# One decoder kernel: the second cross attention as one stream of eight half-batch units

## The chip, the cores and the metric

The kernel runs on one core of one Trainium2 chip. The metric is the time of one launch in microseconds (us), as the device reports it; less is better. TensorE (PE) multiplies, VectorE (DVE), ScalarE (ACT) and GpSimd (POOL) work on the elements, and SyncE (SP) issues the DMAs of this stage. Each engine runs its own list of instructions in order and waits on semaphores for the others.

## The reference

Two decoder layers on 4 batches of 512 tokens with 512 features. Each layer is self attention, cross attention and a feed-forward part, each with its residual and layer norm. The change is in the cross attention of the second layer alone (32 heads of 16 features, context of 256 features):

```python
q = (x @ Wq).reshape(b, n, N_HEADS, HEAD_DIM)
k, v = jnp.split(ctx @ Wkv, 2, axis=-1)
q = apply_axial_rope(q, pos_map)
k = apply_axial_rope(k, ctx_pos_map)
logits = jnp.einsum('bqhd,bkhd->bhqk', q, k) * scale
w = jax.nn.softmax(logits, axis=-1)
attn = jnp.einsum('bhqk,bkhd->bqhd', w, v)
attn = attn.reshape(b, n, N_HEADS * HEAD_DIM)
return attn @ Wout + bout
# afterwards: x = _layernorm(x + ...)
```

## The kernel before

`cross_attention_1` is one stage between two barriers. A loop (`Fori(0, B)` on every engine, B = 4) goes over the batches, and each batch has three parts.

**The head** prepares all 32 heads. PE turns the rows of x and of the context into columns (`turn_tile`, line 116), then projects q tile by tile (L1570) and k and v (L1575). DVE applies the rotary embedding (L1744 to L1749: multiply, two swapped multiplies, add). q and k are split into a high and a low part, since the score matmuls run in the one-pass format fp32r: ACT copies the high part (L1672), and DVE (L1729) and POOL (L1797) subtract to get half of the low part each. PE turns the split rows (L116, "x_ident_r,x_split") and ACT copies them out (L1666) into `q_cols` and `k_cols`, where each head takes 64 rows.

**The steps** are 64 pieces of work that a `plan` orders. One step has the scores of two heads for 128 queries (L1599: two matmuls on the upper and the lower 64 rows of the array, into one pair of PSUM banks) and DVE's row maximum over both banks (L1762). 14 steps later the same two heads are multiplied the other way round (L1618), with the negated maximum in the added rows, and ACT takes the exponential (L1688). Every second step has a "values" piece (L1626: four matmuls of 17 columns side by side in the array). Every 8 steps (a group of four heads) add the turning of the maxima (DVE L1768 and L1770, PE L1608, ACT L1680, four DMAs into `q_cols`) and the way back of the group's result (ACT copy L1693, PE L116, DVE L1776 and L1778). The PSUM banks are two pairs for scores, a ring of three for the weights (a bank is free again when its exponential is done) and one for the values.

**The tail** turns `feats`, multiplies by Wout (L1645), adds the bias (L73), the residual (L77), and normalises (L85 to L96). Only then does the head of the next batch begin.

## Time and profile before

| | us |
|---|---|
| median of 3 runs | 3331.95 (3326.03 to 3333.94) |
| profiled execution: its own time | 3331.01 |
| profiled execution: span | 3329.3 |
| PE busy in the span | 2951.1 (89%) |
| DVE, ACT, POOL busy | 2053.9, 1524.7, 243.0 |
| the changed stage, from 2285.3 to 3014.5 | 729.2 |

The rows are of three kinds: a table of busy times in stretches (here one stretch is one batch, from the first score matmul to the next batch's first); single instructions in order of time, where "x4" joins neighbours of the same kind and the difference of two starts says what a group takes; and groups of equal instructions with their mean duration. A PE duration contains the time through the array, so a group's cost is read from start to start. A plain fp32 matmul shows as two instructions, an fp32r one as one.

### The profile page before, as it was taken

Reading aid. Unit: us, or ns where it says so; the run is one execution under the profiler, and the core shown is the slowest. Engines: PE = TensorE matmul, PEld = TensorE weight load, DVE = VectorE, ACT = ScalarE, POOL = GpSimd, SP = SyncE. Lnnn points to the kernel's source line nnn. Section 1 sums busy time; section 2 is a strip of 40 time slices with the busy share of each in tenths; the row PEclk is TensorE's granted clock in tenths of the full one; section 3 lists DMA queues with packets and bytes.
Section 4 is the critical chain, followed back from the end, with each engine's and each line's share of the span. In section 5 each row is a group of like instructions: output and inputs, shape, how many; then the busy total and the mean of one; then the engine's idle time right before and its main releaser. Section 6 shows DMA issues by size and latency. Waiting matters only on the chain. (4 is left out here: it accounts for less than half of the span.)

```text
span 3329.3 us, 45585 instructions
## 1 busy us (share of the span) xinstructions
PE 2951.1 (89%) x13653; PEld 1768.8 (53%) x13676; DVE 2053.9 (62%) x3875; ACT 1524.7 (46%) x3177; POOL 243.0 (7%) x234
## 2 busy tenths in 40 slices
PE   8999978799999996998998999997898888984787
PEld 4455444336999994655655655654334343432343
DVE  5666645444566565756756856854747575766776
ACT  4445422223555552443543542633556556574444
POOL 0000020002000000101102102101000000000000
PEclk9999989898999998999999999998898989895899
DMA  3000023000000001100000000001000000003000
GB/s 120 13 13 0 13 76 103 31 22 9 12 13 11 11 10 70 76 1 14 1 1 14 1 1 13 1 1 61 2 21 2 21 2 21 2 2 152 7 19 25
DMA packets 43029, 82.10 MB, mean 25 GB/s; under 512 B 6256, under 2 KB 21377, under 8 KB 39393
## 3 DMA queue, kind: packets, MB, share of 16 engines
q1 hardware_dynamic: 39952, 71.60, 6.0%
q0 software_dynamic: 2896, 8.31, 0.8%
q8 instruction: 88, 1.44, 0.2%
q14 instruction: 93, 0.75, 0.1%
HBM read 55.25 MB, written 4.19 MB: 18 GB/s over the span
## 5 line engine op out<-in xcount | busy, mean ns | idle before, releaser
L1232 ACT ACTIVATE a_probs<-bank,a_neg_max 128x128 f32<-128x128 f32 (+3 forms) x256 | 138.6, 542 | 390.6 <-DVE a_neg_max L1335 390.6
L1762 DVE TENSOR_REDUCE x_neg_max<-bank 128x2 f32<-128x1024 f32 x256 | 298.9, 1217 | 28.4 <-PE bank L1599 28.4
L116 PE MATMUL bank<-all_ident,a_probs 128*128 128x128 f32 x1216 | 198.4, 276 | 57.5 <-ACT a_probs_t L1248 39.5
L116 PEld LDWEIGHTS bank<-all_ident,a_probs 128*128 128x128 f32 x1216 | 151.0, 142 | 159.6 <-ACT a_probs L1238 61.5
L1190 PE MATMUL bank<-a_wo,a_att_cols 128*128 128x512 f32 x512 | 226.9, 594 | 1.2 <-DVE a_att_cols L1300 0.9
L955 DVE TENSOR_TENSOR moe_hid_low<-moe_hid,moe_hid_high 128x512 fp32r<-128x512 f32 x168 | 116.3, 692 | 177.1 <-ACT moe_hid_high L825 169.8
L1618 PE MATMUL bank<-x_q_cols,x_k_cols 64*128 64x512 f32 x512 | 160.9, 446 | 35.7 <-ACT x_x_rows L1688 12.7
L753 PE MATMUL bank<-moe_w_high,moe_hid_low 128*128 128x256 f32 x672 | 190.2, 283 | 0.0
L753 PE MATMUL bank<-moe_w_low,moe_hid_high 128*128 128x256 f32 x672 | 190.1, 283 | 0.0
L753 PE MATMUL bank<-moe_w_high,moe_hid_high 128*128 128x256 f32 x672 | 189.3, 282 | 0.1
L1165 PE MATMUL bank<-a_k_cols,a_q_cols 128*128 128x128 f32 (+3 forms) x512 | 176.8, 434 | 0.0
L819 ACT ACTIVATE moe_hid<-bank,moe_b_now 128x512 f32<-128x512 f32 x168 | 115.7, 688 | 122.3 <-PE bank L731 122.3
L1599 PE MATMUL bank<-x_k_cols,x_q_cols 64*128 64x512 f32 x512 | 137.5, 531 | 29.8 <-DVE x_neg_max L1762 21.1
L1131 PE MATMUL bank<-a_x_high,a_w_high 128*128 128x512 f32 x320 | 138.2, 432 | 23.5 <-DVE a_k_cols L1287 11.9
L825 ACT CAST moe_hid_high<-moe_hid 128x512 fp32r<-128x512 f32 x168 | 104.4, 621 | 112.4 <-PE bank L753 112.2
L1190 PEld LDWEIGHTS bank<-a_wo,a_att_cols 128*128 128x128 f32 x512 | 94.2, 190 | 106.6 <-issue 104.4
L1177 PE MATMUL bank<-a_probs_t,a_v_rows 128*128 128x512 f32 (+3 forms) x512 | 148.6, 433 | 0.0
L1238 ACT ACTIVATE a_probs<-a_probs,a_inv_sum 128x128 f32<-128x128 f32 (+3 forms) x256 | 144.8, 565 | 7.6 <-DVE a_inv_sum L1340 7.6
L947 DVE SCALAR_TENSOR_TENSOR moe_acc<-bank,moe_gate_now,moe_acc 128x256 f32<-128x256 f32 x336 | 139.4, 477 | 13.2 <-issue 12.1
L1309 DVE TENSOR_TENSOR all_x_tok<-bank,all_x_tok 128x512 f32 (+1 forms) x64 | 44.2, 691 | 159.6 <-PE bank L1190 159.6
L1335 DVE TENSOR_REDUCE a_neg_max<-bank 128x1 f32<-128x128 f32 (+3 forms) x256 | 125.7, 491 | 19.1 <-issue 0.5
L731 PE MATMUL bank<-moe_gh_high,moe_w_high 128*128 128x512 f32 x336 | 133.7, 398 | 2.1 <-DVEq L938 2.1
(353 smaller groups left out, 6629.2 us busy)
## 6 DMA issues: line engine op xcount, KB each, us to landing
x_x_rows<-all_x_tok SPq DMA_DIRECT2D x8, 1024.0 KB, 6.3
moe_w<-in_L_ffn_e_w SPq DMA_DIRECT2D x40, 128.0 KB, 2.2
all_x_tok<-in_x SPq DMA_DIRECT2D x1, 4096.0 KB, 17.7
x_c_rows<-in_ctx SPq DMA_DIRECT2D x8, 512.0 KB, 4.5
moe_x_rows<-all_x_tok SPq DMA_DIRECT2D x4, 1024.0 KB, 4.7
a_probs<-all_x_tok SPq DMA_DIRECT2D x4, 1024.0 KB, 4.5
a_wqkv<-in_L_attn_Wqkv SPq DMA_DIRECT2D x1, 4096.0 KB, 20.2
a_wo<-in_L_attn_Wo SPq DMA_DIRECT2D x1, 4096.0 KB, 30.0
```

Of the source, the lines that this page charges most:

```text
L116: last = pe.transpose(bank[:, c * P:(c + 1) * P], rows[:, c * P:(c + 1) * P], ident)
L753: last = pe.matmul(to, h[:, c, tokens], weight[:, slot, c, :], start=c == j == n == 0, stop=c == 1 and n == 2, skip_group_check=True)
L947: last = dve.scalar_tensor_tensor(acc[:, t, :], mm[b % 2 * 2 + half][:, j * LATENT:(j + 1) * LATENT], gate_now[:, slot, t:t + 1], acc[:, t ...
L1131: last = pe.matmul(mm[g % 2], weight[:, p % 2, k, :], x[:, k, :], start=n == 0, stop=n == 3 * KD - 1)
L1165: pe.matmul(sc[n % 4][:, 0:t], q_cols[:, h % 2, j * P:t], k_cols[:, h // GROUP, 0:t], start=True, stop=True).then_inc(s.sc.full, 1)
L1177: last = pe.matmul(mm[g % 2][:, c * P:], v_rows[:, c, kv * HD1:(kv + 1) * HD1], probs_t[:, n % 2, c, c * P:], start=c == 0, stop=c == NT - 1)
L1190: last = pe.matmul(mm[g % 2], att_cols[:, h % HALF_HEADS, j * P:(j + 1) * P], wo[:, h, :], start=h == first, stop=h == end - 1)
L1232: act.activation(probs[:, n % SLOTS, 0:t], sc[n % 4][:, 0:t], ACT.Exp, bias=neg_max[:, n:n + 1], accum_out=row_sum[:, n:n + 1]).then_inc(s ...
L1238: act.activation(probs[:, i % SLOTS, 0:t1], probs[:, i % SLOTS, 0:t1], ACT.Copy, scale=inv_sum[:, i:i + 1]).then_inc(s.probs_ready, 1)
L1599: last = pe.matmul(pair_banks[slot % 2][:, u, :], q_cols[rows, pair, j * P:(j + 1) * P], k_cols[rows, pair, :], start=True, stop=True)
L1618: pe.matmul(weight_banks[slot % 3], k_cols[rows, pair, c * P:(c + 1) * P], q_cols[rows, pair, :], start=True, stop=True).then_inc(s.weight ...
L1762: dve.tensor_reduce(neg_max[:, g % 2, j, 2 * pair:2 * pair + 2], pair_banks[slot % 2], AX.X, ALU.max, negate=True) \
```

## The change

The loop over batches is gone. The stage is eight units (u), a half batch of 16 heads each, with 32 steps per unit, all in one `plan` from step -34 on that every engine walks. A unit's steps are as before: scores, weights 14 steps later, values, shift, back. Between them stand the next unit's preparation (v = u + 1): q in two pieces (two tiles of 128 tokens by 256 features each) at steps 0 to 6, k at 8 and 12, v at 16 and 18, the rotary pieces, the "high" (ACT) and "low" (POOL) parts, 16 "pad" turnings at the odd steps from 7 to 17 and at 19 to 25, and the last finished batch's turning of feats, output matmuls and layer norm at steps 20 to 30 of the unit after it and 20 to 27 of the one after that. The last batch's output comes after its last step.

The PSUM banks are dealt anew: a ring of three single banks for scores (so one maximum per head), two for weights (three before), one for values, and two work banks that all preparation shares; a piece takes whichever is emptied first. The buffers of exponentials are two (three before). All of the low part and the bias are POOL's. x is turned straight from `x_tok`, so its reload (1 MB per batch) is gone; the context comes in halves into one buffer, so the second half of batch 0 is loaded behind the weights.

On PE in the steady part, the kernel before, one step with values (x1_k_cols,x1_q_cols are scores; x1_q_cols,x1_k_cols weights):

```order
L1596 REGISTER_ALU
L1599 MATMUL bank<-x1_k_cols,x1_q_cols 128x512 x2
L1617 REGISTER_ALU
L1618 MATMUL bank<-x1_q_cols,x1_k_cols 128x512
L1617 REGISTER_ALU
L1618 MATMUL bank<-x1_q_cols,x1_k_cols 128x512
L1626 MATMUL bank<-x1_x_rows,x1_v_rows 17x512 x4
```

The change, unit 2, steps 22 to 24:

```order
L116 MATMUL bank<-all_ident,x1_feats 128x128 x8
L1704 MATMUL bank<-x1_k_cols,x1_q_cols 128x512 x2
L1715 MATMUL bank<-x1_q_cols,x1_k_cols 128x512 x2
L1737 MATMUL bank<-x1_weights,x1_v_rows 17x512 x4
L116 MATMUL bank<-x1_ident_r,x1_split 128x128 x8
L1704 MATMUL bank<-x1_k_cols,x1_q_cols 128x512 x2
L1715 MATMUL bank<-x1_q_cols,x1_k_cols 128x512 x2
L1663 MATMUL bank<-x1_wout,x1_feats_t 128x512 x2
```

Between scores and weights of neighbouring steps there now stand turnings, projections or output matmuls. On DVE, the kernel before, from the end of one group to its way back:

```order
L1762 TENSOR_REDUCE x1_neg_max<-bank 128x2
L1767 REGISTER_ALU
L1768 CAST x1_shift<-x1_neg_max 128x16
L1770 TENSOR_TENSOR x1_shift<-x1_neg_max,x1_shift 128x16
L1761 REGISTER_ALU
L1762 TENSOR_REDUCE x1_neg_max<-bank 128x2
L1761 REGISTER_ALU
L1762 TENSOR_REDUCE x1_neg_max<-bank 128x2
L1774 REGISTER_ALU
L1776 RECIPROCAL x1_inv_sum<-bank 128x16
L1778 TENSOR_TENSOR x1_feats<-bank,x1_inv_sum 128x4x64
```

The change, steps 9 to 11 of a unit:

```order
L1857 TENSOR_REDUCE x1_neg_max<-bank 128x1 x2
L1875 RECIPROCAL x1_inv_sum<-bank 128x16
L1877 TENSOR_TENSOR x1_feats<-bank,x1_inv_sum 128x4x64
L1899 TENSOR_TENSOR x1_rot<-x1_rot,x1_swapped 128x512
L1890 TENSOR_TENSOR x1_rot<-bank,x1_cos 128x512
L1857 TENSOR_REDUCE x1_neg_max<-bank 128x1 x2
L1894 TENSOR_TENSOR x1_swapped<-bank,x1_sin 128x256 x2
```

The rotary add of q's second piece now stands behind the group's reciprocal, which waits for PE's turning, and two more instructions follow before the next maxima.

The diff, cut to its core:

```diff
-    PAIRS = HEADS // 2
+    UNITS, UH = 2 * B, HEADS // 2
+    UD = UH * HD
+    PAIRS = UH // 2
...
-    SHIFT_SPLIT, SHIFT_TURN = -1, 1
-    T_LAG, V_LAG, BACK_LAG = 14, 2, 4
+    LAG = 14
...
+    first, last_step = -STEPS - 2, STEPS * (UNITS + 2)
+    plan = {i: [] for i in range(first, last_step)}
...
+    for u in range(UNITS):
+        for n in range(STEPS):
+            plan[u * STEPS + n].append(("scores", u, n))
+    for u in range(UNITS):
+        for g in range(GROUPS):
+            plan[u * STEPS + (g + 1) * GS - 1].append(("shift_split", u, g))
+        for n in range(STEPS):
+            plan[u * STEPS + n + LAG].append(("weights", u, n))
+    for u in range(UNITS):
+        for g in range(GROUPS):
+            plan[u * STEPS + (g + 1) * GS + 1].append(("shift_turn", u, g))
+        for n in range(CHUNKS):
+            plan[u * STEPS + LAG + 2 * n + 3].append(("values", u, n))
+        for g in range(GROUPS):
+            plan[u * STEPS + LAG + (g + 1) * GS + 1].append(("copy", u, g))
+            plan[u * STEPS + LAG + (g + 1) * GS + 3].append(("back", u, g))
+
+    def project(piece, where, subs, done):
+
+        for i, step in enumerate(where):
+            for sub in range(i * subs, (i + 1) * subs):
+                plan[step].append(("fill", piece, sub))
+        for kind, step in done:
+            plan[step].append((kind, piece))
...
+    def turn(piece, step):
+        plan[step] += [("fill", piece, 0), ("evac", piece)]
...
+    for v in range(UNITS):
+        at = (v - 1) * STEPS
+        b, hf = divmod(v, 2)
+        if v == 0:
+            prepare_rows(b, at, (-2, -2, -2, -2))
+            prepare_context(b, at, (-1, -1))
+        project(("q", v, 0), (at, at + 2), 2, [("rope_mul", at + 3), ("rope_swap", at + 4), ("rope_add", at + 5), ("high", at + 5), ("low", at + 6)])
+        project(("q", v, 1), (at + 4, at + 6), 2, [("rope_mul", at + 7), ("rope_swap", at + 8), ("rope_add", at + 9), ("high", at + 9), ("low", at + 10)])
+        project(("k", v, 0), (at + 8,), 2, [("rope_mul", at + 9), ("rope_swap", at + 10), ("rope_add", at + 11)])
+        project(("k", v, 1), (at + 12,), 2, [("rope_mul", at + 13), ("rope_swap", at + 14)])
+        for pad, steps in ((0, (7, 9, 11, 13)), (1, (15, 15, 17, 17))):
+            for j, step in enumerate(steps):
+                turn(("pad", v, "q", j, pad), at + step)
+        for kind, step in (("high", 16), ("low", 17)):
+            plan[at + step].append((kind, ("k", v, 0)))
+        plan[at + 15].append(("rope_add", ("k", v, 1)))
+        for kind, step in (("high", 18), ("low", 19)):
+            plan[at + step].append((kind, ("k", v, 1)))
+        for n, step in enumerate((19, 20, 21, 21, 23, 23, 25, 25)):
+            turn(("pad", v, "k", n // 4 * 2 + n % 2, n // 2 % 2), at + step)
+        project(("v", v, 0), (at + 16,), 2, [("value_copy", at + 17)])
+        project(("v", v, 1), (at + 18,), 2, [("value_copy", at + 19)])
+        if hf == 0:
+            for j in range(NT):
+                plan[at + 20 + j].append(("bias", b, j))
+        if hf == 1 and b + 1 < B:
+            prepare_rows(b + 1, at, (9, 11, 13, 13))
+            prepare_context(b + 1, at, (27, 29))
+    for b in range(B):
+        at = (2 * b + 2) * STEPS
+        for j, step in enumerate((20, 20, 22, 22)):
+            turn(("feats", b, j), at + step)
+        late = STEPS if b + 1 < B else 0
+        for j, steps in enumerate(((24, 26), (28, 30), (late + 20, late + 22), (late + 24, late + 26)) if late else ((24, 24), (25, 25), (26, 26), (27, 27))):
+            project(("out", b, j), [at + i for i in steps], 2, [("ln_add", at + steps[-1] + 1)])
+        end = at + (late + 27 if late else 28)
+        plan[end].append(("ln_var", b))
+        for j in range(NT):
+            plan[end + 1 + j // 2].append(("ln_norm", b, j))
...
+            bank = 0 if busy[0] < busy[1] else 1
...
+            work_at[piece[1]] = bank, uses[bank]
+            uses[bank] += 1
+            busy[bank] = consumed[piece[1]]
...
-        weights = [weights_0[:], x_rows[:], scratch[:]]
+        split = sb("split", [P, 2, 2 * UH, PARTS, HD], F32R)
+        weights = sb("weights", [P, 2, GROUP, S])
...
-        pair_banks, weight_banks, value_bank = [m.psum[:, 0:2, :], m.psum[:, 2:4, :]], m.banks[4:7], m.banks[7]
+        score_banks, weight_banks, value_bank, work_banks = m.banks[0:3], m.banks[3:5], m.banks[5], m.banks[6:8]
...
-        s.sc, s.mm, s.pair, s.weight = (Ring(sem, n, size) for n, size in (("sc", 4), ("mm", 2), ("pair", 2), ("weight", 3)))
...
+        s.score, s.weight = Ring(sem, "score", 3), Ring(sem, "weight", 2)
+        s.work = [Ring(sem, f"work_{i}", 1) for i in range(2)]
...
+            def fill(piece, sub):
+                bank = work_bank(piece)
+                ring, use = s.work[work_at[piece][0]], work_at[piece][1]
+                if sub == 0:
+                    pe.wait_ge(ring.free, use + 1)
...
+                elif piece[0] == "pad":
+                    _, v, which, j, pad = piece
+                    source = (which, v, j // 2)
+                    pe.wait_ge(s.low_ready, split_of(source) + 1)
...
+                    turn_tile(pe, bank.bitcast(F32R), rows.rearrange("p h a d -> p (h a d)"), ident_r[:], PW).then_inc(ring.full, 1)
...
+                    for n in (2 * sub, 2 * sub + 1):
+                        j, k = divmod(n, depth)
+                        tokens = slice((2 * half + j) * P, (2 * half + j + 1) * P)
...
+                            x, weight = x_cols[:, k, tokens], wq[:, k, hf * UD:(hf + 1) * UD]
...
+                        last = pe.matmul(bank[:, j * UD:(j + 1) * UD], x, weight, start=k == 0, stop=k == depth - 1)
...
+            for piece in walk():
+                kind = piece[0]
+                if kind == "fill":
+                    fill(*piece[1:])
...
+                    for half in range(2):
+                        slot = score_at[kind, u, n, half]
+                        rows = slice(half * ROWS, (half + 1) * ROWS)
+                        pe.wait_ge(s.score.free, slot + 1)
+                        pe.matmul(score_banks[slot % 3], q_cols[rows, u % 2, pair, j * P:(j + 1) * P], k_cols[rows, u % 2, pair, :],
+                                  start=True, stop=True).then_inc(s.score.full, 1)
...
+                    for half in range(2):
+                        slot = weight_at[kind, u, n, half]
+                        rows = slice(half * ROWS, (half + 1) * ROWS)
+                        pe.wait_ge(s.weight.free, slot + 1)
+                        pe.matmul(weight_banks[slot % 2], k_cols[rows, u % 2, pair, c * P:(c + 1) * P], q_cols[rows, u % 2, pair, :],
+                                  start=True, stop=True).then_inc(s.weight.full, 1)
...
+                    pe.wait_ge(s.shift_ready, u * GROUPS + g + 1)
+                    pe.wait_ge(s.weight.free, slot + 1)
...
+                    _, v, half = piece[1]
+                    p = split_of(piece[1])
+                    act.wait_ge(s.rot_ready, p + 1)
...
+                    act.copy(halves(piece[1])[0], rotated(piece[1], 2)).then_inc(s.hi_ready, 1)
...
+                        act.wait_ge(s.weight.full, slot + 1)
+                        if k == 0 and u * CHUNKS + chunk >= 2:
+                            act.wait_ge(s.chunk_used, u * CHUNKS + chunk - 1)
+                        act.activation(weights[:, chunk % 2, k, :], weight_banks[slot % 2], ACT.Exp).then_inc(s.weight.free, 1)
...
+                    for half in range(2):
+                        slot = score_at[kind, u, n, half]
+                        h = 2 * pair + half
+                        dve.wait_ge(s.score.full, slot + 1)
+                        dve.tensor_reduce(neg_max[:, g % 2, j, h:h + 1], score_banks[slot % 3], AX.X, ALU.max, negate=True) \
+                           .then_inc(s.score.free, 1)
...
+                elif kind in ("rope_mul", "rope_swap", "rope_add"):
...
+                    if kind == "rope_mul":
+                        dve.wait_ge(*filled(piece[1]))
+                        if p >= 2:
+                            dve.wait_ge(s.low_ready, p - 1)
+                        dve.tensor_tensor(tiles(to), bank, cos[:, at:at + 2, :].unsqueeze(2).to_broadcast([P, 2, UH, HD]), ALU.mult)
...
+                elif kind == "ln_add":
+                    _, b, j = piece[1]
+                    x = m.x_tok[:, b * NT + j, :]
+                    dve.wait_ge(*filled(piece[1]))
+                    dve.wait_ge(s.x_biased, b * NT + j + 1)
+                    dve.tensor_tensor(x, work_bank(piece[1]), x, ALU.add).then_inc(s.work[work_at[piece[1]][0]].free, 1)
...
+            for piece in walk():
+                kind = piece[0]
+                if kind == "low":
+                    p = split_of(piece[1])
+                    hi, lo = halves(piece[1])
+                    pool.wait_ge(s.hi_ready, p + 1)
+                    pool.tensor_tensor(lo, rotated(piece[1], 1), hi[:, :, 0:1].bitcast(F32), ALU.subtract).then_inc(s.low_ready, 1)
+                elif kind == "bias":
+                    _, b, j = piece
+                    x = m.x_tok[:, b * NT + j, :]
+                    pool.wait_ge(w_out, 32)
+                    pool.wait_ge(*filled(("x", b, j)))
+                    pool.tensor_tensor(x, x, bout_row[:], ALU.add).then_inc(s.x_biased, 1)
```

## Rows read from the trace of the kernel before

**Rows 1.** Busy us of PE, PEld, DVE, ACT, POOL by stretch; PE clock.

```profile
2285.30:2337.30 52.00, 43.67 (x216) 27.38 (x216) 26.67 (x56) 30.78 (x51) 8.05 (x19) 0.90 0.30 97
2337.30:2516.60 179.30, 160.35 (x840) 71.97 (x840) 114.79 (x161) 105.53 (x197) 7.18 (x9) 0.94 0.03 11
2875.00:2993.80 118.80, 101.91 (x575) 38.64 (x573) 82.28 (x97) 74.56 (x144) 0.00 (x0) 0.91 0.01 2
2993.80:3014.50 20.70, 15.66 (x48) 7.66 (x48) 10.58 (x21) 2.05 (x4) 1.01 (x1) 0.96 0.00 0
```

**Rows 2.** PE in order of time (start, length): two steps; a group's turnings.

```profile
2360.94 0.50 PE L1599 MATMUL bank<-x_k_cols,x_q_cols 64*128 64x512 f32 x2
2361.27 0.39 PE L1618 MATMUL bank<-x_q_cols,x_k_cols 64*128 64x512 f32 x2
2361.51 0.39 PE L1599 MATMUL bank<-x_k_cols,x_q_cols 64*128 64x512 f32 x2
2361.74 0.39 PE L1618 MATMUL bank<-x_q_cols,x_k_cols 64*128 64x512 f32 x1
2362.35 0.50 PE L1618 MATMUL bank<-x_q_cols,x_k_cols 64*128 64x512 f32 x1 [0.22 <-ACT x_scratch L1688]
2362.78 1.05 PE L1626 MATMUL bank<-x_x_rows,x_v_rows 128*17 128x512 f32 x8
2363.76 0.50 PE L1599 MATMUL bank<-x_k_cols,x_q_cols 64*128 64x512 f32 x2
...
2371.55 0.60 PE L1608 MATMUL bank<-all_ident,x_shift 128*8 128x128 f32 x4
2372.08 1.05 PE L1626 MATMUL bank<-x_x_rows,x_v_rows 128*17 128x512 f32 x8
2373.06 0.66 PE L116 MATMUL bank<-all_ident,x_c_rows 128*128 128x128 f32 x4
2373.65 0.50 PE L1599 MATMUL bank<-x_k_cols,x_q_cols 64*128 64x512 f32 x2
```

**Rows 3.** PE in order of time: single fp32r matmuls, another stage.

```profile
899.92 0.40 PE L731 MATMUL bank<-moe_gh_low,moe_w_high 128*128 128x512 f32 x1
900.16 0.39 PE L731 MATMUL bank<-moe_gh_high,moe_w_low 128*128 128x512 f32 x1
```

**Rows 4.** ACT in order of time in the same two steps.

```profile
2361.70 2.06 ACT L1688 ACTIVATE x_scratch<-bank 128x512 f32<-128x512 f32 x4 [1.83 <-PE bank L1618]
```

**Rows 5.** The view of rows 1, ten microseconds of the first batch's ramp.

```profile
2347.00:2357.00 10.00, 8.59 (x28) 4.29 (x29) 9.61 (x12) 2.97 (x6) 0.00 (x0) 0.50 0.01 2
```

**Rows 6.** PE in order of time in the first head.

```profile
2297.58 13.99 PE L1570 MATMUL bank<-x_wq,x_x_cols 128*128 128x512 f32 x32 [0.74 <-ACT x_scratch L1659]
...
2311.01 1.89 PE L116 MATMUL bank<-x_ident_r,x_split 128*128 128x128 f32 x16
2312.74 1.95 PE L1575 MATMUL bank<-x_wkv,x_scratch 128*128 128x512 f32 x4
```

**Rows 7.** DVE in order of time: a way back, then two maxima.

```profile
2373.75 0.26 DVE L1776 RECIPROCAL x_inv_sum<-bank 128x16 f32<-128x16 f32 x1 [1.30 <-PE bank L116]
...
2374.43 2.34 DVE L1762 TENSOR_REDUCE x_neg_max<-bank 128x2 f32<-128x1024 f32 x2
```

**Rows 8.** Groups of equal instructions: busy us, mean ns of one.

```profile
L349 DVE TENSOR_REDUCE a_neg_max<-bank 128x1 f32<-128x512 f32 x128 | 85.6, 687 | 30.4 <-PE bank L236 30.1
...
L1749 DVE TENSOR_TENSOR x_scratch<-x_scratch,x_weights 128x512 f32<-128x512 f32 x32 | 22.1, 692 | 3.0
...
L1672 ACT CAST x_split<-x_scratch 128x1024 fp32r<-128x1024 f32 x32 | 33.9, 1058 | 43.7 <-DVE x_scratch L1749 43.7
```

**Rows 9.** The maxima, all 256: ns min/median/max, first and last start.

```profile
L1762 DVE TENSOR_REDUCE x_neg_max<-bank x256: 1210/1214/1226, 2337.9 to 2968.5; 128x2 f32<-128x1024 f32 x128
```

**Rows 10.** The last weight DMA: its issue in time, its time to landing.

```profile
2290.41 0.68 SPq L1539 DMA_DIRECT2D x_bout_row<-in_L_xattn_bout  x1
...
x_bout_row<-in_L_xattn_bout SPq DMA_DIRECT2D x1, 256.0 KB, 13.0
```

More of the change, by code:

```diff
@@ L1787, in _ @@
                 pool.memset(freq[:, f:f + 1], float(np.float32(ROPE_BASE) ** np.float32(-f / HALF))).then_inc(s.made, 1)
-            pool.memset(v_rows[:, :, :, HD:VALS], 1.0).then_inc(s.ones_ready, 1)
-            for slot in range(SPLIT_SLOTS):
+            for slot in range(2):
                 pool.memset(split[:, slot, :, PARTS - 1, 2:].bitcast(F32), 0.0)
```

550 lines of the change are left out of this document (268 added, 282 removed).

## The prediction

> **What bounds the kernel now.** The change is inside one stage, so I read first the busy time by batch [rows 1]. The stage takes 729.2 us: 52.0 us to the first scores, 179.3 us for each of the first three batches, 118.8 and 20.7 us for the last one's steps and tail. In a batch PE is busy for 160 of 179 us, DVE for 115, ACT for 105. PE is the bound, with 19 us of waiting, all of it in the steps: in the last batch's 118.8 us, which have no head, PE is busy for 101.9.
>
> Next the steps in order of time [rows 2]. Two steps make a cycle of 2.91 us on PE. I write S for a pair of score matmuls, W for a pair of weights, V for values: S .33 (2360.94 to 2361.27), W .24, S .23, then one weights matmul, a wait, the other at 2362.35, V at 2362.78, and V takes .98. A pair of fp32r matmuls goes side by side, two in .24, where a single one takes .23 [rows 2, 3]. A change between this form and the full array costs .09 (S .33 behind V, .24 behind its like). The wait is for a bank of the weight ring: ACT starts its first exponential .43 after its matmul (2361.27 to 2361.70) and PE goes on .65 after that [rows 2, 4]; the second weights matmul to V is another .43. So a cycle is made of ACT's latency and PE's own work in turn, and neither is full. Third, the ramp: while only scores run, PE's granted clock is .50 for ten microseconds, the lower of the two levels, after it idled between score pairs [rows 5]; that happens in each of four batches.
>
> **What the change saves.** The head and tail of a batch are 60 us in which PE does nothing else; the steps' 119 us include a ramp without weights and a drain without scores. The stream puts these together once. The gain would be large if PE's waits were filled, so I add up PE by the unit (half a batch; before it cost 89.6 us).
>
> One double step is S and W, then S, W and V. With other work between them, each S has the .09 in front (.33) and each W, taken in the same way, .10 behind (.34): 2.32 us = 2 x (.33 + .34) + .98, times 16 = 37.1.
> Groups: four turnings of maxima (T, .53) and four ways back (B, .59) [rows 2] = 4.5. T needs the bank of an exponential of its own step, 1.08 (.43 + .65) after W instead of .34. In two of four groups nothing stands between: with .2 for a third, 1.7. Together 6.2.
> Projections: a 128x512 fp32 matmul takes .87 (13.99 us for 16) [rows 6]; q has 16 of half the width and k and v 16: 32 x .43 = 13.7. A pad is four turnings; sixteen take 1.73 [rows 6], so a pad .43, and .5 with the change of form; 16 pads are 8.0.
> Output: 16 x .87 = 13.9 a batch, 7.0 in a unit. Feats 2.0; x and context 3.0 where they stand.
>
> **What the change adds.** (1) The weight ring has two banks. In a double step with no work behind the first W, the second W must wait for both of the first's exponentials: its second matmul starts 1.57 us (.43 + .49 + .65) after the first W, then .43 to V, 2.00 in place of 1.01. That is .99 for each such gap, and a bare cycle is 3.31 where it is 2.91 now. Gaps: 7 in unit 1, 2 in units 2, 4 and 6, 4 in units 3 and 5, 12 in unit 7, 6 in unit 0. (2) Turnings that share one work bank go one after the other: fill, copy, fill; about 1.2 a turn where .5 is counted, .7 more. There are 4 or 5 of them in an even unit (x rows at steps 9 and 13, pads at 17 and 25 while v or output holds the other bank), 2 in an odd one. (3) Step 9. The reciprocal starts .69 after B (2373.06 to 2373.75), .68 go to it and its product, then come the rotary add (.69, behind a drain) and a multiply, all before the maxima of step 10 [rows 2, 7, 8]. ACT stands in "high" (1.05) until the add is done [rows 8], and the exponentials of step 10 queue behind it. I follow that by the rows to a second W of step 11 about 1.1 us late. (4) Maxima: both heads take 1.214 now [rows 9], and two such follow in 2.34, so 1.13 from start to start; one head of 512 columns is .687, so .61 from start to start, 1.22 for two [rows 7, 8]: .09 more a step. DVE comes to 39 for maxima, 5 for groups (.68 for a way back [rows 7], some .6 for a group's end), 9 for rotary pieces, 5 for the rest, some 60 us in a unit: a cover of 15 to 20 us, so (4) costs nothing as long as PE takes over 70. Its waits for B, up to .7 us four times, fit too. (5) POOL's low parts and biases run a step or more before they are needed; no cost.
>
> One rule speaks against this change. A change of form costs .09 now [rows 2]. A weights matmul takes .39 and the next kind starts .24 after it, so .15 of it is still in the array then [rows 2]. If every change waited for that, each of the two changes in 256 steps would cost .06 more, 30 us in all. The Trainium skill, "TensorEngine Tiling (Array Packing)", section Key Properties, says that going to another tiling mode drains TensorE. The row of .09 agrees in kind, not in size; I stay with the row, and the full drain is a rival below.
>
> **Sum by unit.** Unit 2: 37.1 + 6.2 + 13.7 + 8.0 + 7.0 + 2.0 + 3.0 = 77.0; gaps 2.0 and .3 for half-filled ones, shared banks 3.3, step 9 1.1: 83.7. Unit 4 the same. Unit 6 has no x and context: 78.4. Units 3 and 5: 37.1 + 6.2 + 13.7 + 8.0 + 7.0 + 4.0 + 1.5 + 1.1 = 78.6. Unit 1 without output: 73.8. Unit 7 has no next unit: 37.1 + 6.2 + 7.0 + 11.9 = 62.2. Unit 0 has 14 steps without weights, DVE's: 28 x .61 + 3.4 rotary pieces of 2.3 = 25, then 9 double steps with what stands in them, 43: 68. All eight: 607.
> Start: weights and bias have landed by 2290.4 + 13.0 = 2303.4 now [rows 10]; without the reload of x ahead of them some 3 us sooner, and the context's second half comes behind them, about 2301, where now projections start at 2297.6. From there to the first scores is 39.7 now for all heads. Half of PE's work is 20, but the chain rotary, high, low, pads, copies binds: between these ends I take 27, nearer the lower, since half the tiles go through it. First scores at 2328, 43 us.
> Drain: 25.3 now (last maxima at 2968.5 [rows 9], feats at 2993.8), 14 bare steps at .2 more each, 28. Tail: 20.7, as now; the bias add that leaves DVE lay under PE's output matmuls.
> 43 + 607 + 28 + 21 = 699, against 729: 30 us less. The profiled execution's own 3331.0 (span 3329.3 and 1.7 around it) becomes 3301; it lies .9 under the median, so the forecast is **3302 us**.
>
> **Rivals.** *The waits mostly vanish.* Gaps (39 x .99 = 39), T's waits (14), shared banks and step 9 (some 25) come to 78 us. They rest on in-order waiting in my reading; if DVE and ACT run so far behind or ahead that half of it hides, the time is 3263. For: ACT needs only 55 of 80 us. Against: the wait of exactly this kind is there now [rows 2, 4].
> *Slower: pairs fall apart.* Score banks are freed one by one, weight banks too. A pair whose second bank comes late costs .23 more, since its matmuls no longer go side by side. There are 512 pairs; the gain is gone at 130 broken ones, and with half of them broken the time is 3361. For: DVE at 60 of 76 us with bursts of three rotary instructions at steps 3 to 11, where it needs 2.1 us a step, PE 2.15. Against: the second step of a filled cycle comes 1.65 after the first, over the 1.57 that the ring asks.
> *Every change of form drains.* .15 in place of .09 and .10, at 512 changes: 30 us, 3332. For: the rule named above. Against: the .09 [rows 2].
> *The overlap isn't there.* If every engine walks the plan but each preparation waits for its chain, a unit stays at 89.6, with 52 at the start and no second ramps: about 3331, no change.
>
> **Chances.** Forecast .48 (its own range 3282 to 3325: 5% of 607 in either direction is 30, and within it faster .42, same .06), waits vanish .24, pairs .20, full drain .04 and no overlap .04, both the same or a little slower. Faster by over 0.3% (10 us, about what a measurement tells from no change) .66, same .12, slower .22. The range takes in the first rival at half its price, a little beyond, and nearly all of the second: 3255 to 3358.
>
> **What will show it.** PE's start-to-start times: S .33 and W .34 with a projection between, 2.0 from W to V across a gap. Units of 74 to 84 us by the first maxima of each. First scores near 2328. The granted clock at 1.00 from unit 0 on. DVE's mean maximum .69 with waiting on PE rather than PE on DVE. I am wrong if pairs stand .23 apart, if PE waits on DVE's maxima for over 30 us in all, or if step 9 costs more than 2 us.

## The result: 1% slower, where a gain of 1% was forecast

The changed kernel takes 3361.9 us (median of 4 runs, 3359.5 to 3363.4); the kernel before took 3330.1 beside it (4 runs). The ratio is 1.0096, with a 95% interval of 1.0080 to 1.0112. The forecast was 3302 us with a range up to 3358, so both the sign and the range were wrong. The time is near that of the rival "pairs fall apart" (3361), but that mechanism is not what the trace shows.

The profiled execution took 3362.4 us. All of the difference lies in the changed stage: 760.3 us where it was 729.2. The stage as a whole in the view of [rows 1], after the change and then before it:

```profile
2284.00:3044.30 760.30, 667.05 (x3616) 335.87 (x3616) 465.00 (x864) 438.15 (x779) 66.30 (x61) 0.94 0.03 9
```

```profile
2285.30:3014.50 729.20, 641.62 (x3360) 290.14 (x3360) 463.97 (x656) 423.78 (x790) 30.55 (x47) 0.94 0.05 15
```

PE is busy for 25 us more and idle for 6 more (93 where it was 87), at the same mean granted clock, .94.

The busy time by stretch after the change, as in [rows 1]: the start, units 0 to 6 (each from its first scores to the next unit's), the last unit with the drain, and the tail.

```profile
2284.00:2330.74 46.74, 29.91 (x153) 24.25 (x154) 14.06 (x30) 17.49 (x28) 11.56 (x17) 0.83 0.28 91
2330.74:2412.70 81.96, 70.22 (x332) 39.22 (x333) 51.23 (x91) 39.65 (x68) 5.10 (x4) 0.85 0.03 8
2412.70:2488.01 75.31, 69.80 (x420) 35.70 (x417) 53.42 (x98) 51.28 (x92) 10.09 (x8) 1.00 0.01 2
2488.01:2579.17 91.16, 83.12 (x476) 42.39 (x472) 55.05 (x100) 56.79 (x102) 5.12 (x4) 0.94 0.03 7
2579.17:2668.10 88.93, 80.07 (x438) 39.02 (x434) 60.29 (x115) 52.04 (x94) 11.07 (x9) 0.93 0.01 1
2668.10:2758.20 90.10, 82.06 (x472) 41.69 (x472) 54.83 (x99) 56.66 (x102) 5.12 (x4) 0.96 0.02 5
2758.20:2845.80 87.60, 79.13 (x438) 38.35 (x434) 60.35 (x115) 52.04 (x93) 11.08 (x9) 0.94 0.01 2
2845.80:2927.70 81.90, 76.15 (x452) 38.46 (x448) 54.79 (x99) 53.18 (x96) 5.14 (x4) 1.00 0.01 2
2927.70:3025.21 97.51, 82.60 (x432) 30.79 (x428) 52.61 (x103) 58.57 (x109) 1.01 (x1) 0.96 0.01 2
3025.21:3044.30 19.09, 14.00 (x32) 6.00 (x32) 8.35 (x17) 0.44 (x1) 1.01 (x1) 1.00 0.00 0
```

Against the sum of the prediction, in us:

| | forecast | measured | off |
|---|---|---|---|
| start | 43 | 46.7 | +3.7 |
| unit 0 | 68 | 82.0 | +14.0 |
| unit 1 | 73.8 | 75.3 | +1.5 |
| units 2 and 4 | 83.7 each | 91.2, 90.1 | +13.9 |
| units 3 and 5 | 78.6 each | 88.9, 87.6 | +19.3 |
| unit 6 | 78.4 | 81.9 | +3.5 |
| unit 7 and drain | 62.2 + 28 | 97.5 | +7.3 |
| tail | 21 | 19.1 | -1.9 |
| all | 699 | 760.3 | +61.3 |

So the miss is 33 us in units 2 to 5, 14 in unit 0, and 14 spread over the other five rows. Unit 1, which has the lightest filling and stays at clock 1.00, is where the prediction put it.

**What came out as worked out.** PE in order of time after the change, first two filled steps, then an unfilled cycle in the last unit, with the turning of the maxima:

```profile
2416.80 0.60 PE L1724 MATMUL bank<-all_ident,x_shift 128*8 128x128 f32 x4 [0.78 <-ACT x_weights L1809]
...
2418.89 0.50 PE L1704 MATMUL bank<-x_k_cols,x_q_cols 64*128 64x512 f32 x2
2419.23 0.40 PE L1715 MATMUL bank<-x_q_cols,x_k_cols 64*128 64x512 f32 x2
2419.56 1.99 PE L1685 MATMUL bank<-x_wq,x_x_cols 128*128 128x256 f32 x8
2421.48 0.50 PE L1704 MATMUL bank<-x_k_cols,x_q_cols 64*128 64x512 f32 x2
...
2423.13 0.49 PE L1704 MATMUL bank<-x_k_cols,x_q_cols 64*128 64x512 f32 x2
...
2952.11 1.05 PE L1737 MATMUL bank<-x_weights,x_v_rows 128*17 128x512 f32 x8
...
2954.36 0.50 PE L1704 MATMUL bank<-x_k_cols,x_q_cols 64*128 64x512 f32 x1 [0.32 <-DVE x_neg_max L1857]
2954.50 0.98 PE L1715 MATMUL bank<-x_q_cols,x_k_cols 64*128 64x512 f32 x2
2955.41 1.05 PE L1737 MATMUL bank<-x_weights,x_v_rows 128*17 128x512 f32 x8
```

S takes .34 (2418.89 to 2419.23) and W .33 before a projection (forecast .33 and .34); the second step takes 1.65 (2421.48 to 2423.13). The bare cycle is 3.30 from values to values (2952.11 to 2955.41), forecast 3.31. Before the change it was 2.90, from values at 2362.78 [rows 2] to the next:

```profile
2365.68 1.05 PE L1626 MATMUL bank<-x_scratch,x_v_rows 128*17 128x512 f32 x8
```

The forecast had not seen one thing in the bare cycle: the second score matmul waits .32 for DVE's maximum, since the three single banks are not yet free. The cycle came out no longer for it.

**What did not.** The projection takes 1.92 (2419.56 to 2421.48); four matmuls of .43 had been counted, 1.72. And in units 2 and 4 step 9 looks like this, on PE, then ACT, then DVE:

```profile
2512.88 0.54 PE L116 MATMUL bank<-x_ident_r,x_split 128*128 128x128 f32 x4
2515.89 1.12 PE L116 MATMUL bank<-all_ident,all_x_tok 128*128 128x128 f32 x4 [2.47 <-ACT x_q_cols L1777]
2516.94 0.80 PE L1704 MATMUL bank<-x_k_cols,x_q_cols 64*128 64x512 f32 x2
```

```profile
2514.30 1.04 ACT L1793 CAST x_split<-x_rot 128x1024 fp32r<-128x1024 f32 x1 [0.57 <-DVE x_rot L1899]
2515.25 0.59 ACT L1777 ACTIVATE x_q_cols<-bank 128x512 fp32r<-128x512 f32 x1
```

```profile
2513.05 0.42 DVE L1877 TENSOR_TENSOR x_feats<-bank,x_inv_sum 128x256 f32<-128x256 f32 x1
2513.57 0.69 DVE L1899 TENSOR_TENSOR x_rot<-x_rot,x_swapped 128x512 f32<-128x512 f32 x1
```

The chain is the one that the prediction had followed (reciprocal, product, rotary add, "high"). But it went on from "high" to the exponentials only, and missed what stands behind "high" on ACT here: the copy of the pad that PE has just turned. The x turning of the same step wants that pad's work bank, so PE stands for 2.47 us. Behind it PE's granted clock falls: it is .61 in the ten microseconds from 2513, where a pair of scores takes .59 to the next start in place of .34, and .94 over the unit.

The same chain costs something two steps later, in the odd units too. In unit 1 the second score matmul of step 11 waits for a maximum, behind the rotary add and the multiply that stand before the maxima on DVE:

```profile
2440.20 0.50 PE L1704 MATMUL bank<-x_k_cols,x_q_cols 64*128 64x512 f32 x1 [1.20 <-DVE x_neg_max L1857]
```

Step 11 takes 4.8 us there, from its first score matmul to the next step's.

### The profile page after: what moved, and what is told of

Same layout as the page of the kernel before. It is cut to its first block and busy times, and to the rows that moved or that the text cites. A ratio compares the mean times of both kernels' runs of the same rounds, so it can differ in the third digit from the quotient of the medians.

```text
span 3360.3 us, 44342 instructions
## 1 busy us (share of the span) xinstructions
PE 2977.4 (89%) x13932; PEld 1814.6 (54%) x13932; DVE 2057.7 (61%) x4083; ACT 1538.0 (46%) x3166; POOL 278.8 (8%) x248
## 3 DMA queue, kind: packets, MB, share of 16 engines
HBM read 55.25 MB, written 4.19 MB: 18 GB/s over the span
## 5 line engine op out<-in xcount | busy, mean ns | idle before, releaser
L1857 DVE TENSOR_REDUCE x_neg_max<-bank 128x1 f32<-128x512 f32 x512 | 326.4, 683 | 179.9 <-PE bank L1704 179.7
L1809 ACT ACTIVATE x_weights<-bank 128x512 f32<-128x512 f32 x512 | 278.6, 598 | 156.0 <-PE bank L1715 149.5
L1704 PE MATMUL bank<-x_k_cols,x_q_cols 64*128 64x512 f32 x512 | 153.4, 513 | 23.1 <-DVE x_neg_max L1857 22.7
L1715 PE MATMUL bank<-x_q_cols,x_k_cols 64*128 64x512 f32 x512 | 137.5, 433 | 6.9 <-ACT x_weights L1809 6.9
L1737 PE MATMUL bank<-x_weights,x_v_rows 128*17 128x512 f32 x1024 | 141.8, 628 | 0.0
```

The source lines that it names most:

```text
L1704: pe.matmul(score_banks[slot % 3], q_cols[rows, u % 2, pair, j * P:(j + 1) * P], k_cols[rows, u % 2, pair, :], start=True, stop=True).then ...
L1737: last = pe.matmul(value_bank[k * COLS:k * COLS + VALS, :], v_rows[:, u % 2, c, g * GROUP + k, :], weights[:, n % 2, k, :], start=c == 0, ...
L1809: act.activation(weights[:, chunk % 2, k, :], weight_banks[slot % 2], ACT.Exp).then_inc(s.weight.free, 1)
L1857: dve.tensor_reduce(neg_max[:, g % 2, j, h:h + 1], score_banks[slot % 3], AX.X, ALU.max, negate=True) \
```

## The experiments

The ratios are to the kernel before, run beside each (median 3328 to 3333 us).

**One bank less in the kernel before.** The ring of two weight banks alone:

```diff
-pair_banks, weight_banks, value_bank = [...], m.banks[4:7], m.banks[7]
+pair_banks, weight_banks, value_bank = [...], m.banks[4:6], m.banks[7]
```

> Before, with two banks in the weight ring in place of three and nothing else: that part of the change alone. Theory 1 (a bare cycle takes 3.31 in place of 2.91): .40 in each of 128 cycles, 51 us, about 3381. Rival (the ring is not what a bare cycle waits for, DVE's maxima are): under 15 us more, below 3345.

Measured: 3409.2 us, ratio 1.0224 (1.0207 to 1.0241), 76 us more. PE in order of time:

```profile
2377.43 0.51 PE L1599 MATMUL bank<-x_k_cols,x_q_cols 64*128 64x512 f32 x2
...
2378.92 0.98 PE L1618 MATMUL bank<-x_q_cols,x_k_cols 64*128 64x512 f32 x2 [0.53 <-ACT x_x_rows L1688]
...
2380.81 0.50 PE L1599 MATMUL bank<-x_k_cols,x_q_cols 64*128 64x512 f32 x2
```

The cycle is 3.38 in place of 2.90, .48 in 128 cycles or 61 us. The turnings of the maxima are the other user of the ring: in the 24 cycles that hold one the trace grows by .69 (3.50 to 4.19), which is 5 us more. The remaining 10 are not placed. The mechanism holds; 51 us had been expected, so its size was put a third too low.

**The banks dealt back.** After, with three weight banks and two score banks:

```diff
-score_banks, weight_banks, value_bank, work_banks = m.banks[0:3], m.banks[3:5], m.banks[5], m.banks[6:8]
+score_banks, weight_banks, value_bank, work_banks = m.banks[0:2], m.banks[2:5], m.banks[5], m.banks[6:8]
```

> After, with three banks in the weight ring and two in the score ring (as before the change: three weight banks). Theory 1 (the ring of two costs .40 in each of the 39 unfilled cycles, 3.31 against the 2.91 of before, and the maxima's turnings wait less): 16 to 30 us come back, 3332 to 3346, and unfilled cycles measure 2.9. Rival (the score ring binds: DVE takes .68 a maximum and frees its banks one by one, so with two of them score pairs fall apart or wait): no gain or a loss, 3362 or above, with pairs .23 apart at the steps that are filled with rotary pieces.

Measured: 3369.5 us (3357 to 3374), ratio 1.0095 (1.0069 to 1.0120): no gain over the 1.0096 of after, and the expected 3332 to 3346 was missed. Both mechanisms are there at once. PE, in a stretch with a maxima's turning and behind a filled step:

```profile
2418.56 0.40 PE L1715 MATMUL bank<-x_q_cols,x_k_cols 64*128 64x512 f32 x2
2418.89 0.60 PE L1724 MATMUL bank<-all_ident,x_shift 128*8 128x128 f32 x4
...
2421.91 0.50 PE L1704 MATMUL bank<-x_k_cols,x_q_cols 64*128 64x512 f32 x1 [0.42 <-DVE x_feats L1877]
...
2443.41 1.10 PE L1704 MATMUL bank<-x_k_cols,x_q_cols 64*128 64x512 f32 x2 [1.25 <-DVE x_neg_max L1857]
```

The turning of the maxima no longer waits (.33 behind W, where after the change it stood .78 idle), but score pairs now do: .42 for the way back, 1.25 for a maximum. The unfilled cycles did not fall to 2.9 either: the shortest take 3.52 from values to values (before the change 2.90), and 83 of the 256 score pairs start over .2 us apart, where after the change 47 do. With this plan a bank moved from one ring to the other gives nothing.

**Single maxima in the kernel before.**

```diff
-dve.tensor_reduce(neg_max[:, g % 2, j, 2 * pair:2 * pair + 2], pair_banks[slot % 2], ...)
+for u in range(2):
+    last = dve.tensor_reduce(neg_max[:, g % 2, j, 2 * pair + u:...], pair_banks[slot % 2][:, u, :], ...)
```

> Before, with each pair's maxima taken by two instructions of 512 columns in place of one of 1024, in the same two-bank pairs: that part of the change alone. Theory 1 (DVE is not the bound outside the ramps of 14 steps): .15 more a step in 56 ramp steps at most, 0 to 8 us, 3330 to 3341. Rival (DVE's rate sets the steps): .1 to .2 more in each of 256 steps, 25 to 50 us, above 3355.

Measured: 3334.7 us, ratio 1.0015 (1.0005 to 1.0024): 4 us, as theory 1 had it. That part of the change is nearly free.

**The knot of step 9.** After, with "high" of q's second piece a step later:

```diff
-... ("rope_add", at + 9), ("high", at + 9), ("low", at + 10)])
-project(("k", v, 0), (at + 8,), 2, [("rope_mul", at + 9), ("rope_swap", at + 10), ("rope_add", at + 11)])
+... ("rope_add", at + 9), ("high", at + 10), ("low", at + 11)])
+project(("k", v, 0), (at + 8,), 2, [("rope_mul", at + 10), ("rope_swap", at + 11), ("rope_add", at + 12)])
-for pad, steps in ((0, (7, 9, 11, 13)), (1, (15, 15, 17, 17))):
+for pad, steps in ((0, (7, 9, 12, 13)), (1, (15, 15, 17, 17))):
```

> After, with ACT's high part of q's second piece one step later, and the following rotary pieces and one pad with it; nothing else. Theory 1 (at step 9 ACT stands in front of the exponentials waiting for the rotary add, PE idles 2.5 us, and its clock then halves): step 9 of units 2 and 4 falls from 6.6 toward 3, the odd units' step 11 from 6 toward 4, 10 to 20 us less, 3342 to 3352. Rival (the wait only goes to the next step): within 5 us of 3362.

Measured: 3348.8 us (10 runs, 3336.5 to 3360.5), ratio 1.0048 (1.0032 to 1.0064), 13 us less than after. The wait at the same place in unit 2:

```profile
2507.23 0.66 PE L116 MATMUL bank<-all_ident,all_x_tok 128*128 128x128 f32 x4 [0.86 <-ACT x_q_cols L1777]
```

.86 in place of 2.47: the rest is the shared bank. Step 9 went from 6.6 to 4.5, and step 11 of unit 1 from 4.8 to 2.7 (one turning of .47 had moved out of it). In the traces units 0 to 6 take 575.2 us together, where after the change they take 597.0. The ten runs scatter over 24 us, where the four of after lie within 4; the next experiments explain part of that.

**The x turnings in unfilled steps.**

```diff
-prepare_rows(b + 1, at, (9, 11, 13, 13))
+prepare_rows(b + 1, at, (10, 10, 14, 14))
```

> After, with the next batch's four x turnings at steps 10, 10, 14 and 14, which nothing fills, in place of 9, 11, 13 and 13. Theory 1 (turnings that share a bank in one step cost .7 more each, and unfilled steps wait anyway): step 13 of units 0, 2 and 4 falls from 4.8 to about 2.6 and steps 10 and 14 grow by at most .5, some 2 to 3 us in each of three units, 3353 to 3358. Rival (PE's sum of work is the bound and place is indifferent): within 2 us of 3362.

Measured: 3363.2 us (3352.9 to 3369.7), ratio 1.0078 (1.0054 to 1.0102), no gain by the total. But units 0 to 6 took 584.5 us in its trace and 597.0 in that of after. The last unit, the drain and the tail took 132.3 in place of 116.6. The drain alone, from the last scores to the last values, this kernel, then after:

```profile
2985.62:3024.40 38.78, 33.69 (x113) 9.85 (x115) 3.46 (x9) 18.03 (x33) 0.00 (x0) 0.50 0.00 1
```

```profile
2993.40:3019.70 26.30, 21.06 (x115) 6.82 (x115) 3.45 (x9) 18.52 (x35) 0.00 (x0) 1.00 0.00 1
```

The same work takes 38.8 us at a granted clock of .50 and 26.3 at 1.00. One drain cycle takes 3.08 at the full clock, here in after (4.53 at half clock):

```profile
3000.18 0.49 PE L1715 MATMUL bank<-x_q_cols,x_k_cols 64*128 64x512 f32 x2
...
3003.26 0.51 PE L1715 MATMUL bank<-x_q_cols,x_k_cols 64*128 64x512 f32 x2
```

**Fillers.** To tell the clock from the waits, matmuls without a use were put into waits, in banks that are overwritten next. First in the wait of step 9:

```diff
+def busy(count, slot):
+    pe.wait_ge(s.score.free, slot + 1)
+    for _ in range(count):
+        pe.matmul(score_banks[slot % 3], m.ident[:], wq[:, 0, :], start=True, stop=True)
...
+if piece[1] in (("x", 1, 0), ("x", 2, 0), ("x", 3, 0)):
+    busy(3, next_score)
 fill(*piece[1:])
```

> After, with three more fp32 matmuls of 128x512 (2.6 us at full clock) in the wait of step 9 of units 0, 2 and 4, written into the score bank that is overwritten next; they add no result. The wait stays as long as it is. Theory 1 (after these waits PE's granted clock is .5 to .6 for 10 to 20 us and its work there takes twice as long): the clock stays at 1.00 behind them and the steps 10 to 14 there shrink, 8 to 15 us in all, 3347 to 3354. Rival (the low clock comes from something else, or PE is not what binds there): 3360 to 3366.

Measured: 3373.4 us (3361.7 to 3378.3), ratio 1.0126 (1.0102 to 1.0150), slower than both expectations. The profiled drain was at the half clock. Units 0, 2 and 4 had become 7.2 us shorter in all, units 1, 5 and 6 5.9 longer. Then in the drain, on the kernel of high_one_step_later:

```diff
+if u == UNITS - 1 and n % 2 == 0 and n + LAG >= STEPS:
+    busy(1, next_score)
```

> The kernel of high_one_step_later with one fp32 matmul of 128x512 (.87 us at full clock) in the wait between the two weights pairs of each of the drain's seven cycles, written into a free score bank; they add no result. Theory (the last unit and the drain take 94 us at full clock and up to 123 where the granted clock is .5 there, and which of the two a run gets makes its range of 3336 to 3361): the drain stays at full clock, the runs stay within 8 us of each other, median 3337 to 3342. Rival (the clock there has nothing to do with PE's waits, or the filler lies on the path): a median of 3347 to 3356 and a range as wide as before.

Measured: 3339.3 us (7 runs, 3335.6 to 3348.5), ratio 1.0027 (1.0015 to 1.0038). The median came as the theory had it; the runs still lie 13 us apart, where it allowed 8. The drain cycle is 3.08 as without the filler, and the clock 1.00:

```profile
2996.26 0.50 PE L1722 MATMUL bank<-x_q_cols,x_k_cols 64*128 64x512 f32 x2
2996.69 1.13 PE L1692 MATMUL bank<-x_wq,all_ident 128*128 128x512 f32 x2
...
2999.34 0.58 PE L1722 MATMUL bank<-x_q_cols,x_k_cols 64*128 64x512 f32 x2
...
2984.00:3024.00 40.00, 36.42 (x146) 14.15 (x144) 7.49 (x16) 16.03 (x30) 0.00 (x0) 1.00 0.00 1
```

The clock of the drain is not the whole scatter. The traces of high_one_step_later and of this run have the same code up to the drain, the drain at full clock in both, and the same 575 us in units 0 to 6. Yet their executions took 3336.5 and 3345.4 us: the first scores start at 2328.1 in one and at 2336.7 in the other, which is nearly all of the difference.

The same filler on the kernel after itself, and on that with the x turnings moved:

> The kernel after the change with the filler of filler_in_drain and nothing else. Its profiled drain was at full clock already (last unit and drain 105.8 us). If the fillers cost nothing and the drain's clock is what they hold: 3357 to 3363, no change. If the filler lies on the path of each cycle: .3 to .9 in seven cycles, 3364 to 3368.

> The kernel of x_rows_in_gaps with the same filler in the drain. Theory (moving the x turnings took 12 us off units 0 to 6, 585 against 597, and the profiled run lost 17 of it again because its drain ran 50 us at the half clock, 123 against 106): the filler holds the clock and the gain shows, 3344 to 3352, so 8 to 15 under after_drain_filler. Rival (place is indifferent, the 12 us are one run's chance): 3357 to 3363.

Measured: 3362.3 us, ratio 1.0095 (1.0079 to 1.0110), and 3349.6, ratio 1.0053 (1.0038 to 1.0068). So the filler costs nothing that the total shows, and the 12 us that the x turnings had saved now show in the total. The result of x_rows_in_gaps was a gain that a slow drain hid. Last, both fillers on the kernel after:

> The kernel after the change with both fillers, that of step 9 (units 0, 2, 4) and that of the drain. filler_at_step_nine took 7.2 us off units 0, 2 and 4 together, gave 6.0 back in units 1, 5 and 6, and lost the rest in a drain at the half clock. If its gain is real and only the drain hid it: about 7 us under after_drain_filler, 3353 to 3358. If what the clock gives in one place is given back in others: 3359 to 3365, no change.

Measured: 3360.4 us (3356.9 to 3365.6), ratio 1.0094 (1.0080 to 1.0108): the same as without the filler of step 9. The half clock behind that wait costs 2.3 us in unit 2 and 2.4 in unit 4 (88.9 and 88.0 where after_drain_filler has 91.2 and 90.3); units 1 and 5 take 1.4 and 1.5 more, and the total shows nothing. The theory that the clock behind step 9 is worth 8 to 15 us fell. Unit 0 (clock .88) and units 3 and 5 (.93) were not at full clock with the fillers either, so what it costs there was not measured.

**One turning a step.** The plan of high_one_step_later with the same work laid out evenly, and "high" and "low" of k's second piece a step later:

```diff
-for pad, steps in ((0, (7, 9, 12, 13)), (1, (15, 15, 17, 17))):
-    for j, step in enumerate(steps):
-        turn(("pad", v, "q", j, pad), at + step)
+for j, step in enumerate((7, 8, 12, 13)):
+    turn(("pad", v, "q", j, 0), at + step)
+for j, step in enumerate((14, 15, 16, 18)):
+    turn(("pad", v, "q", j, 1), at + step)
-for kind, step in (("high", 18), ("low", 19)):
+for kind, step in (("high", 19), ("low", 20)):
-for n, step in enumerate((19, 20, 21, 21, 23, 23, 25, 25)):
-    turn(("pad", v, "k", n // 4 * 2 + n % 2, n // 2 % 2), at + step)
+for j, pad, step in ((0, 0, 19), (1, 0, 20), (2, 0, 22), (3, 0, 24), (0, 1, 28), (1, 1, 30)):
+    turn(("pad", v, "k", j, pad), at + step)
+for j, step in ((2, 0), (3, 2)):
+    if v > 0:
+        turn(("pad", v - 1, "k", j, 1), at + step)
+    if v == UNITS - 1:
+        turn(("pad", v, "k", j, 1), at + STEPS + step)
-prepare_rows(b + 1, at, (9, 11, 13, 13))
+prepare_rows(b + 1, at, (9, 10, 14, 17))
-for j, step in enumerate((20, 20, 22, 22)):
+for j, step in enumerate((20, 21, 22, 23)):
```

> The kernel of high_one_step_later with the turnings of pads, x rows and feats laid out one to a step, behind a projection's matmuls or in unfilled even steps where there is room, and two of k's pads moved to the first steps of the next unit. Theory (turnings that share a work bank in one step wait .7 for the copy between them, 4.7 us at step 17 and 4.9 to 5.1 at step 25; and a projection's last matmuls take .27 less to the next start when a turning follows, 1.65, than when scores follow, 1.92): steps 17 and 25 fall to about 3.4, 3 to 5 us a unit in seven units, and a sooner start by a few us: 3310 to 3328, under the kernel before. Rival (PE's sum of work binds, the waits only move): 3340 to 3350, like high_one_step_later.

Measured: 3315.3 us (6 runs, 3312 to 3318), ratio 0.9959 (0.9943 to 0.9976): faster than both kernels. It is 33.5 us under high_one_step_later with the same work, but 24.0 under filler_in_drain, the same kernel with its drain held at full clock, and the traces agree with the smaller number: units 0 to 6 take 550.8 us together where high_one_step_later has 575.2. They take 76.0, 71.4, 83.6, 79.0, 82.4, 80.3 and 78.1 us; the prediction had 68, 73.8, 83.7, 78.6, 83.7, 78.6 and 78.4. Units 2 and 3 in the view of [rows 1]:

```profile
2477.03:2560.59 83.56, 79.75 (x478) 40.68 (x474) 54.93 (x100) 56.19 (x103) 5.11 (x4) 0.98 0.03 8
2560.59:2639.56 78.97, 74.32 (x437) 37.24 (x434) 59.61 (x113) 51.28 (x93) 11.07 (x9) 1.00 0.01 2
```

From the first scores to the last values, PE's turnings wait 4.0 us for ACT's copy of an earlier turning where in high_one_step_later they wait 19.6, and the scores wait 13.4 for maxima in place of 21.3. What it removed, in the kernel after, at step 13 of unit 2, where a pad and two x rows share one bank:

```profile
2528.58 0.54 PE L116 MATMUL bank<-x_ident_r,x_split 128*128 128x128 f32 x4
2529.81 0.66 PE L116 MATMUL bank<-all_ident,all_x_tok 128*128 128x128 f32 x4 [0.69 <-ACT x_q_cols L1777]
2531.14 0.66 PE L116 MATMUL bank<-all_ident,all_x_tok 128*128 128x128 f32 x4 [0.68 <-ACT x_x_cols L1760]
```

**More banks where they are idle.** In the drain two score banks join the weight ring, and an odd unit's four normalisations stand one to a step:

```diff
+SPLIT = weight_at["weights", UNITS - 1, STEPS - LAG, 0]
+def weight_bank(slot):
+    if slot < SPLIT:
+        return weight_banks[slot % 2]
+    return (score_banks[0], score_banks[1], weight_banks[SPLIT % 2], weight_banks[(SPLIT + 1) % 2])[(slot - SPLIT) % 4]
...
-plan[end + 1 + j // 2].append(("ln_norm", b, j))
+plan[end + 1 + (j if late else j // 2)].append(("ln_norm", b, j))
```

> The kernel of one_turning_a_step with two of the score banks, which nothing uses after the last scores, added to the two of the weight ring in the drain, and the normalisations of an odd unit one to a step in place of two. Theory (a bare cycle of 3.3 is made of the wait for the two banks): the drain's seven cycles fall to 2.4 to 2.7, 4 to 6 us; steps 28 to 31 of units 3 and 5 lose up to 2 us each; 3306 to 3312. Rival (the drain is bound by ACT's copies and products, not by the banks): 3313 to 3317.

Measured: 3305.2 us (5 runs, 3299.7 to 3307.2), ratio 0.9917 (0.9904 to 0.9931). The drain's cycles, PE in order of time:

```profile
2951.17 1.50 PE L1745 MATMUL bank<-x_q_cols,x_k_cols 64*128 64x512 f32 x4
2953.58 1.05 PE L1745 MATMUL bank<-x_q_cols,x_k_cols 64*128 64x512 f32 x4
2955.55 1.18 PE L1745 MATMUL bank<-x_q_cols,x_k_cols 64*128 64x512 f32 x4
```

2.4 and 2.0 us from cycle to cycle in place of 3.08, the second under the expected 2.4 to 2.7. Ten us for both edits. How they divide was not tried; in the traces the drain from last scores to last values is 7.7 us shorter (19.6 for 27.3), and units 3 and 5 are .9 and 2.3 shorter. This version is the fastest of all, 27 us under the kernel before that ran beside it.

## Why the prediction was wrong

Three steps of the working failed: the price of step 9, the price of a projection or output block, and unit 0 with its clock. Their shares overlap, so they do not add up to the 61 us exactly.

- **The base, S, W, V and the bare cycle** were right to .01 or .02 us, and so was the price of a gap (3.30 for 3.31). The 2.91 for the kernel before is right for its cycles (2.90), but the one cycle that [rows 2] show in full, the first behind the ramp, takes 2.82. The removal of a weight bank from the kernel before gave .48 a cycle where .40 had been worked out. The 3.7 us of the start lie within what the same code shows from trace to trace (first scores from 2328.1 to 2336.7).
- **Step 9** was named, its chain of DVE and ACT was right, and its price was not: 1.1 us forecast, about 3 in units 2 and 4 (6.6 a step, where step 9 of odd units, with one turning less, takes 3.0). The working stopped at the exponentials behind "high"; the pad's copy behind it, for which PE waits with the x turning, was the later one. It also missed that the odd units pay at step 11. The prediction said that it would be wrong "if step 9 costs more than 2 us", and that is one of the ways in which it was. Moving "high" with what follows it gave 13 us by the medians and 22 in units 0 to 6 of the two traces, where 1.1 in each of seven units is 8.
- **The projection blocks** were taken at .43 a matmul. A block before scores takes 1.92 (50 of the 56 in the trace), .20 more than 1.72, and so does an output block (1.91). With 56 + 24 such blocks that is up to 16 us. In the kernel before the projections stood in one row, so [rows 6] could not show it. The cause is argued from the traces, no run was made for it: the last batch's output blocks, one behind the other, go at 1.72 each, and where a turning on the full array follows, a projection block mostly takes 1.64 (19 of 27 in one_turning_a_step, here in high_one_step_later):

```profile
2598.13 1.99 PE L1685 MATMUL bank<-x_wkv,x_c_cols 128*128 128x256 f32 x8
2599.77 0.65 PE L116 MATMUL bank<-x_ident_r,x_split 128*128 128x128 f32 x4
```

So it goes with the change of form. The Trainium skill, "TensorEngine Tiling (Array Packing)", section Key Properties, says that another tiling mode drains TensorE. The prediction had given that rule 4 in 100 and weighed it against a change between the two forms in short matmuls. For those it was right (.33 and .34 measured); behind a full fp32 block the row now agrees with the rule in kind, at .2 to .3.
- **Unit 0** has 14 of the 61 us, the largest single miss. Its first 14 steps were put at 25 us, as DVE's alone; they took 37.5 (2330.74 to 2368.19), and the other 18 took 44.5 where 43 had been reckoned. Step 9 stops PE there too, and the granted clock is .54 in the ten microseconds from 2354:

```profile
2354.78 1.11 PE L116 MATMUL bank<-all_ident,all_x_tok 128*128 128x128 f32 x4 [2.98 <-ACT x_q_cols L1777]
...
2368.19 0.60 PE L1704 MATMUL bank<-x_k_cols,x_q_cols 64*128 64x512 f32 x2
```

One turning a step took the unit to 76.0. The 8 us that remain over 68 were not followed.
- **"The granted clock at 1.00 from unit 0 on"** was wrong: .85 in unit 0, .93 to .96 in units 2 to 5. No term of the sum stood for it, and the stream did not win back the clock of the four ramps: .94 over the stage before and after. The fillers bound its price behind step 9: 2.3 us in unit 2 and 2.4 in unit 4, nothing certain in the total. From the last unit to the end of the stage it is 16 us when the drain runs at half clock (132.3 for 116.6), and the totals of x_rows_in_gaps (3352.9 to 3369.7) suggest that it happens in some runs of a kernel and not in others; no kernel was traced twice.
- **The layer norm** in units 3 and 5 had no term; DVE's instructions were put at nothing. Two bare cycles at the end of each, with layer norm before DVE's maxima, take 4.35 and 4.74 in place of 3.31, some 5 us in all; with one normalisation to a step units 3 and 5 became .9 and 2.3 us shorter. PE's wait in the first of them:

```profile
2660.70 0.49 PE L1704 MATMUL bank<-x_k_cols,x_q_cols 64*128 64x512 f32 x1 [1.75 <-DVE x_neg_max L1857]
```

- **"Turnings that share one work bank ... .7 more each"** held as a term. They were counted as 4 or 5 in an even unit and 2 in an odd one, 17 us in all; from the first scores on, PE's waits for such a copy outside step 9 add up to 17.4 in the trace after the change. What was missed is what goes away with them. The layout with one turning a step gave 24 us: 16 of these waits, 8 of the waits for maxima, and shorter blocks (27 of 56 with a turning behind them, where it was 7), less 5 of a new wait of turnings for the rotary pieces.
- **The rivals.** Pairs do fall apart, but only in part: 47 of the 256 score pairs and 53 of the 256 weights pairs start over .2 us apart, under the 130 that would have cost the gain. PE waited 22.7 us in all for maxima, under the 30 that the prediction had set as its limit, and 21.1 before the change. The rival landed on the measured time by accident. "The waits mostly vanish" is refuted: PE is idle for 93 us of the stage after and 87 before. The same amount of waiting was bought again with other causes, and PE's own work became longer. That is where the gain of one ramp and one drain in place of four went.
- **What held of the argument.** With the knots laid apart, six of seven units come within 2.4 us of the forecast and the kernel gains 15 us on the one before. Part of that agreement is luck: the forecast held 17 us for shared banks, of which this layout has 4 left, and nothing for the blocks, up to 16. The stream itself was sound; its plan was crowded.

## What to carry to other kernels

When a chain of preparation is woven into a pipeline, count for each step how many pieces want the same buffer, and follow the queue of the engine that empties it to its last entry, not to the first that seems to matter. One turning per step was worth 24 us here; a bank moved from one ring to the other was worth nothing. And look at the granted clock of both traces before believing a total: a gain of 12 us was invisible until the drain was held at full clock.

## What the hardware showed

- The same drain took 26.3 us at a granted clock of 1.00 (after) and 38.8 at .50 (x_rows_in_gaps), with the same instructions in the same order. In both traces the clock falls near the last scores, behind a wait of PE of 1.7 us for a maximum; by stretches of ten microseconds after is at 1.00 again from 2994 on, x_rows_in_gaps at .50 up to 3034. What decides it stays open. With a useless matmul in each of the drain's cycles the kernels of x_rows_in_gaps, filler_at_step_nine and high_one_step_later took 14, 13 and 10 us less by the median (8, 11 and 7 by the ratios, each little more than its noise), and the runs of the last of them lie 13 us apart (7 runs) in place of 24 (10 runs). The kernel after, whose traced drain was at full clock already, did not change.
- A full-array fp32 block of eight instructions takes 1.64 from start to start before a full-array turning and 1.92 before a 64-row score pair.
- A useless matmul in a wait is free or nearly so: the drain's cycle stayed at 3.08 us, and the kernel after at 3362.3 with it and 3361.9 without.
